# Second biases of a dense feed-forward: one f32 product of 9 rows, or one bf16 product of 96 rows with nine pairs of parts

## The chip, the cores and the metric

The kernel runs on one core of one Trainium2 chip. The metric is the device time of one execution in microseconds (us), as the median of several runs. The core has five engines that work side by side and meet at semaphores: TensorE (PE; its weight loads are listed apart as PEld), VectorE (DVE), ScalarE (ACT), GpSimd (POOL) and SyncE (SP, which here issues the transfers).

## The reference

The whole reference is a chain of six residual steps on x of 8 x 512 x 256 in f32: an expert feed-forward, an attention, the expert feed-forward again, then a dense feed-forward, a second attention, and the dense feed-forward again. The change lies in the dense feed-forward alone, which is run twice with the same weights (E = 8 experts, H = 128, D = 256, K = 2):

```python
scores = jax.nn.sigmoid(x @ gate_W) * route_scale
topk_scores, topk_idx = jax.lax.top_k(scores, K)
topk_w = topk_scores / topk_scores.sum(-1, keepdims=True)
gate_full = jnp.einsum('bsk,bske->bse', topk_w, jax.nn.one_hot(topk_idx, E))
h = jax.nn.gelu(jnp.einsum('bsd,edh->bseh', x, W1) + b1, approximate=False)
y = jnp.einsum('bseh,ehd->bsed', h, W2) + b2
expert_out = jnp.einsum('bse,bsed->bsd', gate_full, y)
shared = jax.nn.gelu(x @ Ws1 + bs1, approximate=False) @ Ws2 + bs2
return expert_out + shared
```

It is called as `x = x + 0.5 * ffn(layernorm(x))`. Every expert is computed for every token and weighted by its gate, which is zero for six of the eight. What matters here is the term of the second biases: for each token, the sum over experts of gate times `b2`, and the shared expert's `bs2`.

## The kernel before, in words

The residual x stays in on-chip memory (`core.x`) throughout. The kernel is a row of phases, one for each step of the reference, each a block with an instruction list for each engine; a barrier of all engines stands between two phases. The dense feed-forward is `ffn1_phase`, the fourth and the last phase. Phase A below is its first run, phase B the second.

A phase takes the 8 batches of 512 tokens in turn. The loop runs over pairs of batches, with two buffers (k = 0, 1) for what is kept per batch. The shared expert counts as a ninth (NE = 9), and `RUN` puts it first. In the loop TensorE does this for each n from 0 to 8:

- `up`: two f32 products of 128 x 512 for the next expert (L299), on which ScalarE applies gelu (L360);
- `down`: four f32 products of 128 x 256 for expert n (L311), one for each tile of 128 tokens, into two halves of the buffers `y_ps`. There are four such buffers, so TensorE can be two experts ahead of VectorE; `y_free` says which are free;
- between them: at n = 2 `turn_gates`, four transposes of the batch's gates (L289); at n = 4 and 5 the transposes of the next batch's normalised x (L164); at n = 6 the next batch's gate logits (L281).

After n = 8 come the `biases` (L324): for each tile of tokens one product of the turned gates (9 rows) with `b2_sb` (9 rows: b2, and bs2 with the gate 0.5), and then the first `up` of the next batch.

VectorE adds each y, times its gate, to x: `add(n)` (L428 for four tiles, L422 for the shared expert and the biases, two halves each). Behind `add(0)` it takes the statistics of the next batch, behind `add(2)` it copies the turned gates out of the accumulator (L411) and normalises the next batch (L149, L152), behind `add(4)` and `add(5)` it copies its transposes (L176), behind `add(7)` it computes its gates (L384 to L406). `add(8)` and `add(9)`, the biases, close the batch. Instructions of an engine run in the order of its list.

Ahead of the loop SP issues all loads of weights (L246 to L258), VectorE normalises batch 0 and computes its gates, `gates(0, 0)`, and TensorE makes the transposes, the first `up` and the logits of batch 0, then waits for the loads and enters the loop. Also in the last batch of a phase the work for the next batch is done, on spare tiles, and nothing of it is used.

Of the kernel before, what the change touches and what calls it, by code (L numbers as in the profile page):

```python
# [185 lines left out]
def ffn1_phase(core, name, gate_w, w1, b1, w2, b2, ws1, bs1, ws2, bs2, route_scale, out_dram=None):  # L186

    nc = core.nc  # L190
# [4 lines left out]
    YB = 4  # L195
    ctx = ExitStack()
    with ctx:
# [8 lines left out]
        b2_sb = sb("b2", [NE, D])  # L206
# [11 lines left out]
        gate_t = [sb(f"gate_t{k}", [NE, S]) for k in range(2)]  # L218
# [11 lines left out]
        const_ready = sem("const_ready")  # L230
        logits_ready = sem("logits_ready")
        sig_ready = sem("sig_ready")
        gate_ready = sem("gate_ready")
# [11 lines left out]
        def _(sp):  # L245
# [11 lines left out]
            sp.dma_start(b2_sb[0:E, :], b2).then_inc(down_loaded, 16)  # L257
            sp.dma_start(b2_sb[E:NE, :], bs2.rearrange("(o d) -> o d", o=1)).then_inc(down_loaded, 16)  # L258
# [6 lines left out]
        @block.gpsimd  # L265
        def _(pool):
            nc.gpsimd.iota(iota_e[:, :, :], pattern=[[0, TPB], [1, E]], base=0, channel_multiplier=0,
                           allow_small_or_imprecise_dtypes=True)
            for k in range(2):
                last = nc.gpsimd.memset(gate[k][:, :, E:NE], 0.5)  # L270
            last.then_inc(const_ready, 1)

        @block.tensor
        def _(pe):
# [11 lines left out]
            def turn_gates(i, k):  # L286
                pe.wait_ge(gate_ready, i + 1)
                for j in range(TPB):
                    last = nc.tensor.transpose(gate_ps[0:NE, j * P:(j + 1) * P], gate[k][:, j, :],  # L289
                                               core.ident[:, :])  # L290
                last.then_inc(gate_t_ready, 1)
# [25 lines left out]
            def biases(i, k):  # L317
                pe.wait_ge(gate_t_copied, i + 1)
                for half in range(2):
                    m = 2 * NE + half  # L320
                    pe.wait_ge(y_free, i * UNITS + m + 1)
                    for j in range(2):
                        t = 2 * half + j
                        last = nc.tensor.matmul(y_ps[m % YB][:, j, :], gate_t[k][:, t * P:(t + 1) * P],  # L324
                                                b2_sb[:, :], start=True, stop=True)
                    last.then_inc(y_ready, 1)
# [7 lines left out]
            pe.wait_ge(down_loaded, 64)  # L334
            with pe.Fori(0, B // 2) as pair:
                for k in range(2):
                    i = pair * 2 + k
                    for n in range(NE):
                        if n + 1 < NE:
                            up(i, k, n + 1)  # L340
                        down(i, k, n)
                        if n == 2:
                            turn_gates(i, k)
                        if n in (4, 5):
                            norm.pe_transpose(i + 1, chunks=(n - 4,))
                        if n == 6:
                            logits(i + 1, 1 - k)
                    biases(i, k)
                    up(i + 1, 1 - k, 0)
# [30 lines left out]
        def _(dve):  # L380
            def gates(i, k):
# [20 lines left out]
                for r in range(2):  # L402
# [4 lines left out]
                                        ALU.add).then_inc(gate_ready, 1)  # L407

            def copy_gates(i, k):
                dve.wait_ge(gate_t_ready, i + 1)  # L410
                nc.vector.tensor_copy(gate_t[k][:, :], gate_ps[0:NE, :]).then_inc(gate_t_copied, 1)  # L411
# [29 lines left out]
            gates(0, 0)  # L441
            for i in range(1, B):
                core.wait_x(dve, i)
            with dve.Fori(0, B // 2) as pair:
                for k in range(2):
                    i = pair * 2 + k
                    for n in range(NE + 1):
                        add(i, k, n)
                        if n == 0:
                            norm.dve_stats(i + 1)  # L450
                        if n == 2:
                            copy_gates(i, k)
                            norm.dve_normalise(i + 1)
                        if n in (4, 5):
# [2220 lines left out]
```

## Time and profile before

| | |
|---|---|
| median of 3 runs | 3226.8 us (3223.7 to 3229.19) |
| profiled execution, its own time | 3219.98 us |
| its span, first to last instruction | 3218.2 us |
| mean granted TensorE clock | 0.947 of full |
| busy share of the span: PE, PEld | 90%, 64% |
| busy share: DVE, ACT, POOL | 51%, 47%, 42% |
| start of phase A, of phase B (first load issued) | 2018.22 us, 2904.87 us |

A busy share is an average over six phases with different limits; the place of the change is the last phase and the fourth. Times in the rows below are microseconds from the span's start, unless marked as ns. An f32 product stands in the trace as two records on PE.

### The profile page before, as it was taken

To read this page: it belongs to the slowest core of one execution; us is meant where nothing else is said; L and a number is where in the kernel's file an instruction comes from. 1 tells how busy PE (TensorE), PEld (TensorE's weight loads), DVE (VectorE), ACT (ScalarE), POOL (GpSimd) and SP (SyncE) were. 2 spreads that over 40 slices of the span, in tenths; PEclk is the share of its full clock that TensorE was granted. 3 is DMA by queue.
4 is the path that set the end of the run, shared out by engine and by line. 5 is a ranking of instruction groups with operands and counts; after the bars stand their busy time and mean duration, and the time that the engine had idled before them with its cause. 6 is when DMAs were issued, how large, how long until landed. Compare 5 with 4: busy or idle time off the path is not lost. (4 is left out here: it accounts for less than half of the span.)

```text
span 3218.2 us, 53908 instructions
## 1 busy us (share of the span) xinstructions
PE 2896.9 (90%) x19497; PEld 2067.5 (64%) x19497; DVE 1649.1 (51%) x4513; ACT 1527.6 (47%) x2577; POOL 1346.6 (42%) x1333
## 2 busy tenths in 40 slices
PE   5899999768999999568999999899969999998999
PEld 4799999733444443247999998566635666655666
DVE  4411111168888888455111111566676666665666
ACT  1133333249988888410333332233347777772332
POOL 3444444359989888335344443000043344320000
PEclk9899999989999999757999999899989999998999
DMA  7199999713544444641899997200052233301000
GB/s 278 40 302 317 321 316 319 239 30 20 61 60 60 59 59 60 94 168 53 262 319 321 322 313 236 82 0 0 8 142 72 70 88 95 95 2 37 13 13 20
DMA packets 354987, 431.81 MB, mean 134 GB/s; under 512 B 84528, under 2 KB 312771, under 8 KB 350659
## 3 DMA queue, kind: packets, MB, share of 16 engines
q1 hardware_dynamic: 330178, 395.16, 44.2%
q0 software_dynamic: 24576, 33.57, 4.8%
q8 instruction: 144, 2.36, 0.3%
q14 instruction: 89, 0.72, 0.1%
HBM read 355.80 MB, written 72.88 MB: 133 GB/s over the span
## 5 line engine op out<-in xcount | busy, mean ns | idle before, releaser
L1674 ACT ACTIVATE f_h_t<-f_h_ps,f_b_t 128x128 f32<-128x128 f32 x1024 | 320.4, 364 | 617.1 <-PE f_h_ps L1633 617.1
L2041 POOL TENSOR_TENSOR a_dmg_buf<-a_c 128x2048 f32<-128x2048 f32 x128 | 520.1, 4096 | 65.6 <-PE a_dmg_ps L2088 43.9
L1633 PEld LDWEIGHTS f_h_ps<-f_rows_t,f_w 128*128 128x128 f32 x4096 | 481.5, 193 | 9.9 <-issue 3.5
L1633 PE MATMUL f_h_ps<-f_rows_t,f_w 128*128 128x128 f32 x4096 | 482.6, 276 | 2.3 <-DVE f_rows_t L1686 1.2
L1644 PE MATMUL f_y_ps<-f_w,f_h_t 128*128 128x256 f32 x2048 | 462.9, 379 | 0.0
L1593 POOL DMA_INDIRECT acc_rows<-f_y,f_give x128 | 205.0, 1602 | 509.1 <-DMA acc_rows<-f_y,f_give 372.1
L1644 PEld LDWEIGHTS f_y_ps<-f_w,f_h_t 128*128 128x128 f32 x2048 | 379.3, 190 | 46.4
L2373 DVE SCALAR_TENSOR_TENSOR a_bond_buf<-a_a,a_small_rep,a_q_ps 128x512 f32<-128x512 f32 x512 | 346.9, 741 | 36.8 <-PE a_bond_ps L2088 35.1
L428 DVE SCALAR_TENSOR_TENSOR x_resid<-f_y_ps,f_gate,x_resid 128x256 f32 x512 | 218.7, 479 | 162.5 <-PE f_y_ps L311 156.9
L885 ACT ACTIVATE a_prob<-a_prob,a_neg_top 128x384 f32<-128x384 f32 (+3 forms) x512 | 276.5, 570 | 47.3 <-POOL a_neg_top L702 46.9
L299 PE MATMUL f_h_ps<-f_xn_t,f_w 128*128 128x512 f32 x584 | 282.5, 611 | 3.3 <-DVE f_xn_t L176 1.8
L998 DVE CUSTOM_DVE_ANT_0 a_prob<-a_s_ps,a_factor 128x384 f32<-128x384 f32 (+3 forms) x512 | 234.4, 486 | 86.5 <-PE a_s_ps L779 84.5
L360 ACT ACTIVATE f_h_t<-f_h_ps,f_b 128x512 f32<-128x512 f32 x146 | 100.3, 687 | 368.6 <-PE f_h_ps L299 368.3
L311 PEld LDWEIGHTS f_y_ps<-f_w,f_h_t 128*128 128x128 f32 x1152 | 219.6, 191 | 86.2 <-issue 55.1
L311 PE MATMUL f_y_ps<-f_w,f_h_t 128*128 128x256 f32 x1152 | 270.5, 380 | 0.1
L1686 DVE COPY f_rows_t<-f_t_ps 128x256 f32<-128x256 f32 x128 | 54.4, 425 | 408.4 <-PE f_t_ps L1621 408.4
L2309 ACT ACTIVATE a_dmg_buf<-a_dmg_buf,a_small_rep 128x2048 f32<-128x2048 f32 x128 | 255.2, 1994 | 4.9 <-POOL a_dmg_buf L2041 4.8
L2304 ACT ACTIVATE a_bond_buf<-a_bond_buf,a_bond_act_b 128x2048 f32<-128x2048 f32 x128 | 255.5, 1996 | 2.0 <-DVE a_bond_buf L2373 1.8
L1693 DVE TENSOR_TENSOR f_y_biased<-f_y_ps,f_b 128x256 f32<-128x256 f32 x128 | 54.4, 425 | 393.4 <-PE f_y_ps L1644 381.3
L790 PE MATMUL a_t_ps<-ident,a_prob 128*128 128x128 f32 x1280 | 231.1, 280 | 17.6 <-ACT a_prob_t L896 13.5
L896 ACT COPY a_prob_t<-a_t_ps 128x512 f32<-128x512 f32 (+1 forms) x352 | 192.8, 548 | 100.7 <-PE a_t_ps L790 99.5
L702 POOL TENSOR_SCALAR a_neg_top<-a_top 128x1 f32<-128x1 f32 x512 | 105.1, 209 | 323.5 <-DVE a_top L998 298.5
(333 smaller groups left out, 4274.5 us busy)
## 6 DMA issues: line engine op xcount, KB each, us to landing
f_w<-in_L_ffn_w_dram SPq DMA_DIRECT2D x256, 1024.0 KB
a_skewed<-skew SPq DMA_DIRECT2D x8, 2048.0 KB, 8.4
a_k_s<-parts SPq DMA_DIRECT2D x16, 768.0 KB, 7.8
acc_rows<-x_resid SPq DMA_DIRECT2D x17, 512.0 KB, 4.5
xn_rows<-f_xn SPq DMA_DIRECT2D x16, 512.0 KB, 3.0
x_resid<-acc_rows SPq DMA_DIRECT2D x16, 512.0 KB, 7.5
a_vals<-val_rows SPq DMA_DIRECT2D x64, 128.0 KB, 5.3
skew<-a_bond SPq DMA_DIRECT2D x32, 256.0 KB
```

Source lines behind the costliest of these rows:

```text
L299: last = nc.tensor.matmul(h_ps[(k * NE + n) % 2][:, :], w1_sb[:, RUN[n], c, :], norm.xn_t[k][:, c, :], start=c == 0, stop=c == DC - 1)
L311: last = nc.tensor.matmul(y_ps[m % YB][:, j, :], h[:, t * P:(t + 1) * P], w2_sb[:, RUN[n], :], start=True, stop=True)
L790: last = nc.tensor.transpose(t_ps[pack % TB][:, col + kb * P:col + (kb + 1) * P], prob[:, u % PR, kb * P:(kb + 1) * P], core.ident[:, :])
L885: nc.scalar.activation(prob[:, u % PR, 0:width], prob[:, u % PR, 0:width], ACT.Exp, bias=neg_top[:, u % PR:u % PR + 1]).then_inc(exp_ready, 1)
L998: nc.vector.tensor_tensor_reduce(out=prob[:, u % PR, 0:width], in0=s_ps[use % SB][:, 0:width], in1=factor[:, S - width:S], scale=1.0, scal ...
L1633: last = nc.tensor.matmul(h_ps[n // HB][:, (n % HB) * P:(n % HB + 1) * P], w1_sb[s][:, c, n * P:(n + 1) * P], rows_t[e % 2][:, c, :], star ...
L1644: last = nc.tensor.matmul(y_ps[k][:, 0:D], h_t[k][:, n, :], w2_sb[e % R][:, n, :], start=n == 0, stop=n == HC - 1)
L1674: nc.scalar.activation(h_t[k][:, n, :], h_ps[n // HB][:, (n % HB) * P:(n % HB + 1) * P], ACT.Gelu, bias=b1_t[:, n, e:e + 1]).then_inc(gelu ...
L2041: nc.gpsimd.tensor_tensor(dmg_buf[n % RING][:, :, :], places(c_sb[h], first_place(dg)), c_sb[h][:, PAD:].unsqueeze(1).broadcast_to([P, DG, ...
L2304: nc.scalar.activation(buf[:, :, :], buf[:, :, :], ACT.Gelu, bias=bond_act_b[:, h:h + 1]).then_inc(bond_act, 1)
L2309: nc.scalar.activation(buf[:, :, :], buf[:, :, :], ACT.Gelu, bias=small_rep[:, B_DAMAGE:B_DAMAGE + 1]).then_inc(dmg_act, 1)
L2373: last = nc.vector.scalar_tensor_tensor(out=bond_buf[n % RING][:, dd, :], in0=a_sb[h][:, d + 1:d + 1 + S], scalar=small_rep[:, POS + d:POS ...
```

## The change

The bias product is made in bf16. An f32 number is the sum of three bf16 parts (the rounded number, the rounded rest, the rest of that), and the product of a gate and a bias is the sum of nine products of parts. These nine pairs are laid out as rows of one product: group m of 32 rows holds part m of the biases, three times over (27 rows, 5 of zeros), and in `gate_parts` each group has the three parts of the gates. So the product has 96 rows in the place of 9. What this asks for:

- SP: b2 and bs2 are loaded nine times each, 18 loads in the place of 2, behind a wait for GpSimd, which first sets `b2_sb` to zero (and `gate_parts`).
- VectorE, once per phase, behind `gates(0, 0)`: `split_biases`, which waits for the 18 loads and makes `b2_rows` in seven operations. TensorE waits for it ahead of the loop.
- VectorE, per batch: `split_first` behind the statistics at n = 0 and `split_second` at n = 1, seven operations on 36 or 108 columns.
- TensorE: `turn_gates` transposes 96 columns in the place of 9, at n = 3 in the place of n = 2; the copy L411 moves to n = 3 with it and writes bf16.

```diff
-        b2_sb = sb("b2", [NE, D])
+        b2_sb = sb("b2", [PROWS, D])
+        b2_rest = sb("b2_rest", [PROWS, D])
+        b2_part = sb("b2_part", [PROWS, D], BF16)
+        b2_rows = sb("b2_rows", [PROWS, D], BF16)
...
-            sp.dma_start(b2_sb[0:E, :], b2).then_inc(down_loaded, 16)
-            sp.dma_start(b2_sb[E:NE, :], bs2.rearrange("(o d) -> o d", o=1)).then_inc(down_loaded, 16)
+            sp.wait_ge(b2_cleared, 1)
+            for m in range(PARTS):
+                for l in range(PARTS):
+                    row = 32 * m + NE * l
+                    sp.dma_start(b2_sb[row:row + E, :], b2).then_inc(b2_loaded, 16)
+                    sp.dma_start(b2_sb[row + E:row + NE, :], bs2.rearrange("(o d) -> o d", o=1)).then_inc(b2_loaded, 16)
...
+            nc.gpsimd.memset(b2_sb[:, :], 0.0).then_inc(b2_cleared, 1)
+            nc.gpsimd.memset(gate_parts[:, :, :], 0.0)
...
-            def turn_gates(i, k):
-                pe.wait_ge(gate_ready, i + 1)
+            def turn_gates(i):
+                pe.wait_ge(parts_ready, i + 1)
                 for j in range(TPB):
-                    last = nc.tensor.transpose(gate_ps[0:NE, j * P:(j + 1) * P], gate[k][:, j, :],
+                    last = nc.tensor.transpose(gate_ps[0:PROWS, j * P:(j + 1) * P], gate_parts[:, j, :],
                                                core.ident[:, :])
...
-                        last = nc.tensor.matmul(y_ps[m % YB][:, j, :], gate_t[k][:, t * P:(t + 1) * P],
-                                                b2_sb[:, :], start=True, stop=True)
+                        last = nc.tensor.matmul(y_ps[m % YB][:, j, :], gate_t[:, t * P:(t + 1) * P],
+                                                b2_rows[:, :], start=True, stop=True)
...
-            pe.wait_ge(down_loaded, 64)
+            pe.wait_ge(down_loaded, 32)
+            pe.wait_ge(b2_split, 1)
...
-                        if n == 2:
-                            turn_gates(i, k)
+                        if n == 3:
+                            turn_gates(i)
...
-            def copy_gates(i, k):
+            def copy_gates(i):
                 dve.wait_ge(gate_t_ready, i + 1)
-                nc.vector.tensor_copy(gate_t[k][:, :], gate_ps[0:NE, :]).then_inc(gate_t_copied, 1)
+                nc.vector.tensor_copy(gate_t[:, :], gate_ps[0:PROWS, :]).then_inc(gate_t_copied, 1)
+
+            def split_biases():
+                dve.wait_ge(b2_loaded, 32 * PARTS * PARTS)
+                nc.vector.tensor_copy(b2_part[:, :], b2_sb[:, :])
+                nc.vector.drain()
+                nc.vector.tensor_copy(b2_rows[0:32, :], b2_part[0:32, :])
+                nc.vector.tensor_tensor(b2_rest[:, :], b2_sb[:, :], b2_part[:, :], ALU.subtract)
+                nc.vector.drain()
+                nc.vector.tensor_copy(b2_part[:, :], b2_rest[:, :])
+                nc.vector.drain()
+                nc.vector.tensor_copy(b2_rows[32:64, :], b2_part[32:64, :])
+                nc.vector.tensor_tensor(b2_rest[:, :], b2_rest[:, :], b2_part[:, :], ALU.subtract)
+                nc.vector.drain()
+                nc.vector.tensor_copy(b2_rows[64:PROWS, :], b2_rest[64:PROWS, :]).then_inc(b2_split, 1)
+
+            def split_first(k):
+                nc.vector.tensor_copy(gate_part[0][:, :, :], gate[k][:, :, :])
+                nc.vector.drain()
+                nc.vector.tensor_tensor(gate_rest[:, :, :], gate[k][:, :, :], gate_part[0][:, :, :], ALU.subtract)
+                nc.vector.tensor_copy(place_part(0), across(gate_part[0][:, :, :]))
+                nc.vector.drain()
+                nc.vector.tensor_copy(gate_part[1][:, :, :], gate_rest[:, :, :])
+
+            def split_second():
+                nc.vector.drain()
+                nc.vector.tensor_tensor(place_part(2), across(gate_rest[:, :, :]), across(gate_part[1][:, :, :]), ALU.subtract)
+                nc.vector.tensor_copy(place_part(1), across(gate_part[1][:, :, :])).then_inc(parts_ready, 1)
...
             gates(0, 0)
+            split_biases()
...
                         if n == 0:
                             norm.dve_stats(i + 1)
+                        if n == 0:
+                            split_first(k)
+                        if n == 1:
+                            split_second()
                         if n == 2:
-                            copy_gates(i, k)
                             norm.dve_normalise(i + 1)
+                        if n == 3:
+                            copy_gates(i)
```

`place_part(l)` is the place of part l in all three groups of `gate_parts`, `across` repeats a part over the groups; PARTS = 3 and PROWS = 96.

## Rows read from the trace of the kernel before

**Rows 1.** The page: granted TensorE clock in 40 equal slices, in tenths

```profile
PEclk9899999989999999757999999899989999998999
```

**Rows 2.** The page: the chain that ended last, shares of the span by line

```profile
PE f_h_ps L299 4%; PE f_y_ps L311 4%; PE f_gate_ps L281 1%; PE f_y_ps L324 0%; PE f_tp L164 0%; PE f_gate_ps L289 0%; DVE x_resid L428 0%; DVE f_xn_t L176 0%; DVE f_xn L152 0%; DVEq L458 0%; DVE f_stats L134 0%; DVEq L415 0%; DVE f_top_i L390 0%; DVEq L385 0%; DVEq L135 0%
```

**Rows 3.** Windows: length, busy by engine (instructions), granted clock, DMA share, GB/s

```profile
2920.00:2926.00 6.00, 5.91 (x11) 2.92 (x11) 2.46 (x23) 4.14 (x5) 0.00 (x0) 0.53 0.00 0
2119.80:2156.00 36.20, 36.20 (x146) 24.68 (x145) 23.76 (x76) 11.72 (x15) 0.00 (x0) 1.00 0.00 0
```

**Rows 4.** Timeline, turn of a batch: start, duration, engine, line, shapes, count, idle before

```profile
2069.10 1.99 PE L324 MATMUL f_y_ps<-f_b,f_gate_t 9*128 9x256 f32 x8
...
2071.02 3.70 PE L299 MATMUL f_h_ps<-f_xn_t,f_w 128*128 128x512 f32 x8
...
2073.14 1.29 DVE L422 SCALAR_TENSOR_TENSOR x_resid<-f_y_ps,x_resid 128x512 f32 x2 [0.17 <-issue]
...
2074.56 1.89 PE L311 MATMUL f_y_ps<-f_w,f_h_t 128*128 128x256 f32 x8
```

**Rows 5.** Timeline, the last batch of phase B

```profile
3213.01 1.29 DVE L422 SCALAR_TENSOR_TENSOR x_resid<-f_y_ps,x_resid 128x512 f32 x2 [0.17 <-issue]
```

**Rows 6.** Timeline, the start of phase A (SPq: SP issues a transfer)

```profile
2027.10 2.11 SPq L257 DMA_DIRECT2D f_b<-in_L_ffn_b_dram  x1
2027.36 0.17 POOL L267 IOTA f_iota_e<- 128x32 f32 x1 [19.20 <-issue]
...
2029.25 0.25 SPq L258 DMA_DIRECT2D f_b<-in_L_ffn_bs_dram  x1
...
2034.97 3.54 PE L299 MATMUL f_h_ps<-f_xn_t,f_w 128*128 128x512 f32 x4 [1.58 <-DMA f_b<-in_L_ffn_bs_dram]
...
2037.78 0.19 DVE L406 TENSOR_TENSOR f_gate<-f_part 128x32 f32<-128x32 f32 x1
```

**Rows 7.** Timeline, the start of phase B

```profile
2911.47 0.25 SPq L258 DMA_DIRECT2D f_b<-in_L_ffn_bs_dram  x1
...
2919.88 3.76 PE L299 MATMUL f_h_ps<-f_xn_t,f_w 128*128 128x512 f32 x4
...
2924.41 0.19 DVE L406 TENSOR_TENSOR f_gate<-f_part 128x32 f32<-128x32 f32 x1
```

**Rows 8.** Timeline, bf16 products and a bf16 weight load of other phases

```profile
1510.79 0.49 PE L1329 MATMUL f_pos_ps<-f_pick,f_before 128*128 128x256 bf16 x3
...
1511.11 0.67 PE L1333 MATMUL f_pos_ps<-f_pick,f_ones 128*128 128x192 bf16 x9
...
2600.84 0.10 PEld L777 LDWEIGHTS a_s_ps<-a_k_s,a_q_s 96*128 96x128 bf16 x1
```

**Rows 9.** Timeline, VectorE: first and last of seven splitting operations; four of L152

```profile
24.87 0.18 DVE L1431 CAST f_gate_b_part<-f_gate_b 3x64 bf16<-3x64 f32 x1 [5.41 <-DMA f_gate_b<-in_L_ffn_gate_b_dram]
...
26.32 0.27 DVE L1442 SCALAR_TENSOR_TENSOR f_gate_b_rows<-f_gate_b_rest,ident,f_gate_b_sum 3x64 bf16<-3x64 f32 x1
...
2084.99 1.38 DVE L152 TENSOR_SCALAR f_xn<-x_resid,f_mean_var,f_rstd 128x256 f32 x4
```

**Rows 10.** Timeline, VectorE at n = 2 of the second batch

```profile
2082.51 1.74 DVE L428 SCALAR_TENSOR_TENSOR x_resid<-f_y_ps,f_gate,x_resid 128x256 f32 x4 [1.48 <-PE f_y_ps L311]
```

**Rows 11.** One of ten small loads in a row; landing times of L246; the DMA list

```profile
644.93 0.42 SPq L1931 DMA_DIRECT2D a_small<-in_L_attn_w_damage_dram  x1
```

```profile
DMA to landing us min/median/max: 2.1/4.7/7.3
```

```profile
f_b<-in_L_ffn_bs_dram SPq DMA_DIRECT2D x2, 0.5 KB, 4.1
```

**Rows 12.** Timeline, four transposes with 9 and with 128 columns of weights

```profile
2046.96 0.60 PE L289 MATMUL f_gate_ps<-ident,f_gate 128*9 128x128 f32 x4
...
2054.29 0.60 PE L164 MATMUL f_tp<-ident,f_xn 128*128 128x128 f32 x4
```

**Rows 13.** Timeline, the start of the first expert's products

```profile
148.42 6.46 PE L1633 MATMUL f_h_ps<-f_rows_t,f_w 128*128 128x128 f32 x32 [0.61 <-DVE f_rows_t L1686]
```

More of the change, by code:

```diff
@@ L195, in ffn1_phase @@
     YB = 4
+    PARTS = 3
+    PROWS = 32 * PARTS
     ctx = ExitStack()
@@ L217, in ffn1_phase @@
         gate = [sb(f"gate{k}", [P, TPB, NE]) for k in range(2)]
-        gate_t = [sb(f"gate_t{k}", [NE, S]) for k in range(2)]
+        gate_part = [sb(f"gate_part{l}", [P, TPB, NE], BF16) for l in range(2)]
+        gate_rest = sb("gate_rest", [P, TPB, NE])
+        gate_parts = sb("gate_parts", [P, TPB, PROWS])
+        gate_t = sb("gate_t", [PROWS, S], BF16)
         h_t = [sb(f"h_t{k}", [P, S]) for k in range(2)]
@@ L230, in ffn1_phase @@
         const_ready = sem("const_ready")
+        b2_cleared = sem("b2_cleared")
+        b2_loaded = sem("b2_loaded")
+        b2_split = sem("b2_split")
+        parts_ready = sem("parts_ready")
         logits_ready = sem("logits_ready")
         sig_ready = sem("sig_ready")
-        gate_ready = sem("gate_ready")
         gate_t_ready = sem("gate_t_ready")
@@ L406, in gates @@
                 nc.vector.tensor_tensor(gate[k][:, :, 0:E], part[0][:, :, :], part[1][:, :, :],
-                                        ALU.add).then_inc(gate_ready, 1)
-            def copy_gates(i, k):
+                                        ALU.add)
+            def copy_gates(i):
                 dve.wait_ge(gate_t_ready, i + 1)
-                nc.vector.tensor_copy(gate_t[k][:, :], gate_ps[0:NE, :]).then_inc(gate_t_copied, 1)
+                nc.vector.tensor_copy(gate_t[:, :], gate_ps[0:PROWS, :]).then_inc(gate_t_copied, 1)
@@ new lines, in place_part, with across @@
+            def place_part(l):
+                return gate_parts[:, :, :].rearrange("p j (m r) -> p j m r", m=PARTS)[:, :, :, l * NE:(l + 1) * NE]
+            def across(part):
+                return part.unsqueeze(2).broadcast_to([P, TPB, PARTS, NE])
+            def split_first(k):
[5 more added lines that the diff above has]
+                nc.vector.tensor_copy(gate_part[1][:, :, :], gate_rest[:, :, :])
```

## The prediction

> **What bounds the kernel now.** I read the page first. The granted clock of TensorE is at nine or ten tenths in almost all slices [rows 1], and the chain that ended last is made of TensorE lines: L299 and L311 with 4% each, L281 with 1%, and L324, the bias product, below that [rows 2]. This chain is the last phase only. A barrier stands ahead of each phase, so a feed-forward phase counts in full, and there are two dense ones: phase A from 2018 us and phase B from 2905 us.
>
> Then the windows: over one batch of 36.2 us TensorE is busy for all 36.20 us at full clock, VectorE for 23.76 us and ScalarE for 11.72 us [rows 3]. Inside the loop the path is TensorE's own work, and the others have slack. Outside it are two places that the averages hide: the start of each phase, where the loop waits for loads or runs straight on, and the end, where VectorE finishes. So the timeline is needed for three stretches: the turn from one batch to the next [rows 4], the last additions [rows 5] and the two starts [rows 6, 7].
>
> **1. The bias products themselves (a gain).** L324 starts at 2069.10 and the next products (L299) at 2071.02, so the block takes 1.92 us: eight records, since an f32 product is two [rows 4]. In bf16 with 96 rows it is four. The bf16 product nearest to it in the trace has 256 columns as well: three of L1329 start at 1510.79 and the next line at 1511.11, 0.11 us each [rows 8]. The two waits in the block leave about 0.2 us (1.92 less 8 x 0.215, the pace of L311, 1.73 us for eight starts in the same rows). So 4 x 0.11 + 0.2 = 0.64 us, and the gain is 1.28 us. Bounds: if each weight load of 0.10 us [rows 8] stood ahead of its product, 1.04 us, a gain of 0.88; if the waits vanish too, 0.44 us, a gain of 1.48. The shortest reading is no surer than the longest, so I take the middle.
>
> How often does it count? In all batches but the last of each phase. There VectorE closes: its chain add(7), gates, add(8), add(9) doesn't start from the bias product but from add(7), and add(9) begins at 3213.01 right behind add(8), with 0.17 us of issue and no wait for TensorE [rows 5]. Biases that are ready 1.3 us sooner end nothing sooner. So 14 batches, not 16: 14 x 1.28 = **17.9 us gained** (12.3 to 20.7).
>
> At the turn the pipeline must also follow. VectorE ends add(9) at 2074.43 and now gets its next product from L311, which starts at 2074.56 [rows 4]; 1.28 us sooner it has the first half ready at about 2074.2, so VectorE starts some 0.3 us behind its data. TensorE doesn't wait for that, because it may run two experts ahead (four y_ps buffers, two per expert): over 4 us of lead.
>
> **2. Turning the gates.** Four transposes with 96 columns of weights in the place of 9. Four transposes with 128 take 0.60 us, as do the four with 9 [rows 12]: nothing. Moving them from n = 2 to n = 3 moves the same work to the same engine: nothing, as long as the split is done by then. The copy at L411 has the same 512 columns, and goes behind add(3) with them.
>
> **3. VectorE's splitting in the loop.** Seven small operations and three more waits for the pipeline to drain. The trace has their like: the three parts of the expert gate's bias, seven operations on 64 columns, take from 24.87 to 26.59, 1.7 us [rows 9], so some 1.5 us per batch: about 0.9 behind the statistics at n = 0 and 0.6 at n = 1. VectorE has 12 us idle per batch [rows 3], but at n = 0 and 1 it is already late. It waits again at n = 2, for 1.48 us [rows 10], so a lag of 1.5 us is used up there, and n = 2 has lost its gate copy. The cover is the lead of over 4 us; I put the cost at **0** (0 to 1). Were the cover gone, each further us per batch would cost 14.
>
> **4. The start of each phase (a loss).** The loop now waits on TensorE for b2_split: 18 loads in SP's queue instead of 2, then a split that stands in VectorE's queue behind gates(0, 0). Nothing overlaps it, since TensorE's queue has only the loop behind the wait. SP waits for a memset on GpSimd ahead of the loads. If that is as late as GpSimd's first instruction in A is now, 2027.36, it costs 0.6 us against 2027.10, when SP comes to the loads [rows 6]; if it runs at the phase's start, nothing, which I take.
>
> - *Loads.* In A the first pair is issued at 2027.10 (2.11 us, behind the large weights) and 2029.25 [rows 6]. Small loads in a row take 0.42 us each [rows 11] and 0.04 between two, as behind the first pair, 0.46 us, so the last begins at 2029.25 + 16 x 0.46 = 2036.6. Landing: between 2.1 us, the least of L246, and 4.1 us, the median of the small f_b load [rows 11]; I take 3.0, hence 2039.6. In B: 2911.47 + 7.4 + 3.0 = 2921.8 [rows 7].
> - *A page beside it.* The Trainium skill ("DMA: Bandwidth & Descriptors", the section on the anatomy of one DMA) gives a fixed cost of about 2.0 us per transfer. By it A's last load lands at 2038.6, and the whole change would come out 1 us better, as an estimate; the 4.1 us of the row speaks for more.
> - *Gates.* They end at 2037.97 in A [rows 6] and 2924.60 in B [rows 7]. So A waits for the loads, B for VectorE.
> - *Split.* Seven operations on 256 columns with four drains. The 1.7 us above is for 64 columns; a 256-column operation takes 0.345 us (L152, 1.38 for four [rows 9]) and would make 7 x 0.345 + 0.3 = 2.7 us; casts and copies may be cheaper. I take 2.6 (1.8 to 3.0), with 0.2 us of semaphores in all.
> - *Sum.* A: 2039.6 + 2.8 = 2042.4, where the loop starts at 2034.97 today [rows 6]: 7.4 us lost. With loads at 0.29 us each the gates end last: 2037.97 + 0.2 + 1.8, 5.0 us lost; with 4.1 us of landing and 3.0 of split 8.9. B: 2924.6 + 2.8 = 2927.4, where it starts at 2919.88 without a wait: 7.5 us lost (6.7 to 8.0). **14.9 us lost** (11.7 to 16.9).
>
> **5. The clock at the start.** The granted clock is 0.53 in B from 2920 to 2926 [rows 3], mostly the lower level of 1.2 GHz, and the four L299 records at the start take 3.54 us in A [rows 6] and 3.76 in B [rows 7] against half that in the loop. TensorE runs below its level for some 3 us in A and 6 us in B before it rises, so today this costs about 1.5 + 3 = 4.5 us. It will stand idle longer, and start again at the lower level: the idle stretch takes nothing more, but the rise may come sooner or later. Another dense start has 32 records of 128 columns in 6.46 us [rows 13], 0.20 us each, where 256 columns take 0.215 in the loop: 6.5 us at the lower level, a cost of 3.2. Twice 1.5 to twice 3.2 against 4.5: **0** taken, -1.5 to +1.9.
>
> **Sum.** -17.9 + 14.9 + 0 + 0 = -3.0 us. On the profiled execution, 3219.98 us (span 3218.2), this gives 3217.0. The median of the runs is 6.8 us above that execution, so I add the difference to the median: 3226.8 - 3.0 = **3223.8 us**. All ends on one side: -20.7 + 11.7 - 1.5 = -10.5, 3216.3; on the other -12.3 + 16.9 + 1.9 + 1 = +7.5, 3234.3. A measurement of this kernel can tell about 0.2%, 6.5 us, from no change.
>
> **Rivals.**
> - *Faster: the loads and the split are short, and the products retire without breaks.* 14 x 1.48 = 20.7 gained, 5.0 + 6.7 lost: -9.0, 3217.8 us. For it: the last load of a row is issued in 0.25 us, and casts may be quick. Against it: the b2 loads sit in a row of loads, where 0.46 us is the rule. Chance 0.17.
> - *Slower: SP's issue of b2.* L257 takes 2.11 us in A [rows 6]. I read it as a queue still full of weights. If it is its own cost, and only 1.4 of it stays, eight further pairs take 1.4 + 0.3 each: the last is issued at 2029.25 + 13.6 = 2042.9 in A and at 2925.1 in B, and with the same 3.0 and 2.8 us behind it the loop starts at 2048.7 and 2930.9: 13.7 and 11.0 us lost. 24.7 - 17.9 = +6.8, 3233.6 us. It decides from about 1.4 us for each b2 load. Against it: small loads of many rows in rows 11 take 0.42. Chance 0.09.
> - *VectorE becomes the bound at n = 1 to 3.* Needs a lag over 4 us, three times what I find; at half a us per batch over that, +7 on my sum: 3231. Chance 0.03.
> - *The bf16 products cost what the f32 ones do.* Then only the loss is left: 3241.7. Rows 8 speak against it. Chance 0.02.
>
> **How the numbers follow.** My forecast holds 0.69. It spreads from 3218 to 3231 by itself, with some of that below the bound for faster and little above the one for slower. Faster: 0.17 and 0.03 of mine, 0.20. Slower: 0.09 + 0.02 + 0.01, 0.12. Same: 0.68. Range: from the faster rival to the SP rival, 3217 to 3233.5.
>
> **What the profile after would show.** L324 with 64 records in all, bf16, 96 rows, and 0.6 to 0.7 us from it to the next L299; a batch of 34.9 us; 16 more SP issues at about 0.46 us; the loop's first L299 at 24 us after A's first issue (2018.2) where it is 16.8 now, and 22.5 after B's (2904.9) where it is 15.0; add(0) right behind add(9); no wait of TensorE for x_resid at n = 2 or 3. I am wrong if the batch is not near 34.9 us, if a start costs more than 10 us, or if TensorE waits for parts_ready.

## The result and the profile after

| | median | lowest to highest | runs |
|---|---|---|---|
| before | 3223.22 us | 3213.24 to 3231.72 | 20 |
| changed | 3211.81 us | 3200.91 to 3223.45 | 20 |

The ratio is 0.9965 with a 95% interval of 0.9953 to 0.9976. By the ratio that is 11.3 us less (7.7 to 15.2), more than the 0.2% that can be told from no change. The forecast was 3223.8 us, from 3217.0 to 3233.5, with 0.68 on no change. Of the 12.0 us between forecast and result, 3.6 come from the base, since 20 runs put the kernel before at 3223.2 and not at 3226.8. The other 8.4 are the change itself: the medians differ by 11.4 where 3.0 was said. The profiled execution took 3202.66 us, with a span of 3200.9.

The page of the changed kernel, part 4, answers to [rows 2]: the chain is still TensorE's, and the bias product (L344) has sunk within it from fourth to sixth place.

```profile
PE f_h_ps L319 4%; PE f_y_ps L331 4%; PE f_gate_ps L301 0%; PE f_tp L164 0%; PE f_gate_ps L309 0%; PE f_y_ps L344 0%; DVE x_resid L483 0%; DVE f_xn_t L176 0%; DVE f_xn L152 0%; DVE f_top_i L411 0%; DVEq L519 0%; DVE f_stats L134 0%; DVEq L470 0%; DVE f_top_v L408 0%; DVEq L445 0%
```

**The turn of a batch.** The timeline of TensorE over the same turn as [rows 4], then its weight loads.

```profile
2065.55 3.62 PE L331 MATMUL f_y_ps<-f_w,f_h_t 128*128 128x256 f32 x16
2069.00 0.60 PE L344 MATMUL f_y_ps<-f_b_rows,f_gate_t 96*128 96x256 bf16 x4
2069.44 3.60 PE L319 MATMUL f_h_ps<-f_xn_t,f_w 128*128 128x512 f32 x8
2072.88 1.89 PE L331 MATMUL f_y_ps<-f_w,f_h_t 128*128 128x256 f32 x8
```

```profile
2065.55 3.21 PEld L331 LDWEIGHTS f_y_ps<-f_w,f_h_t 128*128 128x128 f32 x15 [0.24 <-issue]
2068.79 0.53 PEld L344 LDWEIGHTS f_y_ps<-f_b_rows,f_gate_t 96*128 96x128 bf16 x4
2069.33 0.30 PEld L319 LDWEIGHTS f_h_ps<-f_xn_t,f_w 128*128 128x128 f32 x2
```

The same stretch of the kernel before, in rows that the first part did not show: the last products ahead of the biases, and the weight loads around them.

```profile
2065.56 3.62 PE L311 MATMUL f_y_ps<-f_w,f_h_t 128*128 128x256 f32 x16
```

```profile
2069.10 1.59 PEld L324 LDWEIGHTS f_y_ps<-f_b,f_gate_t 9*128 9x128 f32 x8 [0.33 <-issue]
2071.02 0.30 PEld L299 LDWEIGHTS f_h_ps<-f_xn_t,f_w 128*128 128x128 f32 x2 [0.33 <-issue]
```

Compare starts, not durations. Before, the steps from the last L311 block to the biases, to L299 and to the next L311 are 3.54, 1.92 and 3.54 us. After, they are 3.45, 0.44 and 3.44. The block itself fell by 1.48 us, and each neighbour is 0.1 us shorter as well, which together makes 1.67. The weight loads show the border. The first bias load used to begin with its own product at 2069.10 after 0.33 us of idle, and now begins 0.21 us ahead of it, with no idle. The next line's load used to have another 0.33 us ahead of it, and that is gone as well. The other seven loads of the old block had none: over all 128 loads of L324 the trace of the kernel before counts 16 such idles, 5.3 us, one for each of the 16 blocks. So the cost stands where the number of rows changes, from 128 to 9 and back, and not at each load of 9 rows.

The period confirms it. Here is the timeline of the next two bias blocks, and the window over one batch (length, busy by engine, granted clock, as in [rows 3]):

```profile
2103.54 0.60 PE L344 MATMUL f_y_ps<-f_b_rows,f_gate_t 96*128 96x256 bf16 x4
2138.07 0.60 PE L344 MATMUL f_y_ps<-f_b_rows,f_gate_t 96*128 96x256 bf16 x4
```

```profile
2133.50:2168.04 34.54, 34.54 (x141) 23.78 (x141) 24.61 (x81) 11.72 (x16) 0.00 (x0) 1.00 0.00 0
```

The bias blocks follow each other at 34.53 and 34.54 us throughout both phases, where they followed at 36.21 before. TensorE is busy for the whole of a batch, so nothing in it waits for VectorE, though VectorE has 0.85 us more work (24.61 against 23.76).

VectorE at the same turn and at n = 0 to 2: the additions follow one another, the splitting lies between them, and the third addition no longer waits 1.48 us for TensorE as in [rows 10].

```profile
2073.11 1.29 DVE L477 SCALAR_TENSOR_TENSOR x_resid<-f_y_ps,x_resid 128x512 f32 x2 [0.17 <-issue]
2074.67 1.29 DVE L477 SCALAR_TENSOR_TENSOR x_resid<-f_y_ps,x_resid 128x512 f32 x2 [0.28 <-issue]
...
2077.89 0.17 DVE L456 CAST f_gate_part<-f_gate 128x36 bf16<-128x36 f32 x1
...
2078.53 0.18 DVE L461 CAST f_gate_part<-f_gate_rest 128x36 bf16<-128x36 f32 x1
...
2080.63 0.27 DVE L465 TENSOR_TENSOR f_gate_parts<-f_gate_rest,f_gate_part 128x108 f32<-128x108 f32 x1
2080.81 0.21 DVE L466 CAST f_gate_parts<-f_gate_part 128x108 f32<-128x108 bf16 x1
2081.19 1.66 DVE L483 SCALAR_TENSOR_TENSOR x_resid<-f_y_ps,f_gate,x_resid 128x256 f32 x4 [0.16 <-issue]
```

**The start of phase A** (first issue at 2013.54), to be held against [rows 6]: the first two and the last of the eighteen loads, the logits block, the end of gates(0, 0), the first and the last of the seven splitting operations, and the loop's first products.

```profile
2013.54 0.37 SPq L259 DMA_DIRECT2D f_w<-in_L_ffn_Ws_dram  x1
2013.55 0.31 POOL L285 MEMSET f_b<- 96x256 f32 x1 [10.69 <-POOLq L51]
...
2021.90 1.40 SPq L274 DMA_DIRECT2D f_b<-in_L_ffn_b_dram  x1
...
2023.64 0.27 SPq L274 DMA_DIRECT2D f_b<-in_L_ffn_b_dram  x1
...
2025.24 1.85 PE L301 MATMUL f_gate_ps<-f_gate_w,f_xn_t 128*128 128x8 f32 x16
...
2028.21 0.25 SPq L275 DMA_DIRECT2D f_b<-in_L_ffn_bs_dram  x1
...
2031.48 0.19 DVE L427 TENSOR_TENSOR f_gate<-f_part 128x32 f32<-128x32 f32 x1
2031.59 0.28 DVE L436 CAST f_b_part<-f_b 96x256 bf16<-96x256 f32 x1
...
2033.65 0.28 DVE L446 CAST f_b_rows<-f_b_rest 32x256 bf16<-32x256 f32 x1
2034.29 3.77 PE L319 MATMUL f_h_ps<-f_xn_t,f_w 128*128 128x512 f32 x4 [7.19 <-DVE f_b_rows L446]
```

The load rows show that the loads are not what the loop waits for. From the second pair on they take 0.27 and 0.25 us, the last is issued at 2028.21, and the split begins at 2031.59, right behind the gates. TensorE's wait of 7.19 us is released by the last splitting operation. The loop starts 20.75 us after the phase's first issue here and 16.8 us after it before. Phase B does the same, as its timeline shows beside [rows 7]:

```profile
2894.55 0.39 SPq L259 DMA_DIRECT2D f_w<-in_L_ffn_Ws_dram  x1
...
2912.47 0.19 DVE L427 TENSOR_TENSOR f_gate<-f_part 128x32 f32<-128x32 f32 x1
...
2915.28 3.78 PE L319 MATMUL f_h_ps<-f_xn_t,f_w 128*128 128x512 f32 x4 [7.36 <-DVE f_b_rows L446]
```

**The balance.** From the first issue of phase A to that of the phase behind it is 310.8 us before and 303.7 after. From the first issue of phase B to the end of the span it is 313.3 and 306.3. So the two phases gave 14.1 us in this profile. The terms are 14 x 1.67 = 23.4 gained, 4.0 and 5.7 lost at the starts, and 0.3 gained between the loop's start and its steady pace. The span fell by 17.3. The other 3.2 us lie in code that the change doesn't touch, and are scatter of the profiled executions.

### The profile page after: what moved, and what is told of

It is laid out like the page before. It is cut to its first block and busy times, and to the rows that moved or that the text cites. A ratio compares the mean times of both kernels' runs of the same rounds, so it can differ in the third digit from the quotient of the medians.

```text
span 3200.9 us, 53982 instructions
## 1 busy us (share of the span) xinstructions
PE 2868.0 (90%) x19433; PEld 2047.2 (64%) x19433; DVE 1667.3 (52%) x4623; ACT 1526.7 (48%) x2577; POOL 1348.1 (42%) x1337
## 5 line engine op out<-in xcount | busy, mean ns | idle before, releaser
L319 PE MATMUL f_h_ps<-f_xn_t,f_w 128*128 128x512 f32 x584 | 280.8, 608 | 16.3 <-DVE f_b_rows L446 14.6
L851 PE MATMUL a_t_ps<-ident,a_prob 128*128 128x128 f32 x1280 | 232.4, 281 | 17.3 <-ACT a_prob_t L957 13.3
```

Source lines behind the costliest of these rows:

```text
L319: last = nc.tensor.matmul(h_ps[(k * NE + n) % 2][:, :], w1_sb[:, RUN[n], c, :], norm.xn_t[k][:, c, :], start=c == 0, stop=c == DC - 1)
L851: last = nc.tensor.transpose(t_ps[pack % TB][:, col + kb * P:col + (kb + 1) * P], prob[:, u % PR, kb * P:(kb + 1) * P], core.ident[:, :])
```

## The experiments

Ahead of each result stands what was expected of it. The first four ran on one chip, where one run of the kernel before took 3232.81 us.

**after_again.** The changed kernel once more, with no edit, to see how far two of its executions differ.

> The changed kernel once more, for what varies by itself. Inside a phase the batch should be 34.54 us again and the loop should start 20.7 us after the phase's first issue. Theory 1: the logits ahead of the loop ran at full clock by the luck of when the clock rose (block of 16 records 1.85 us where it was 3.42 before): then the block may take either length here, and the loop's start lies between 20.7 and 22.4. Theory 2: it belongs to the change: 1.85 again in both phases.

It took 3214.08 us. The period is 34.53 to 34.54 us again, so the gain in the loop is the same. The starts are not: the loop begins 22.4 us after A's first issue (at 2023.70) and 22.5 after B's (at 2903.94), 1.6 and 1.8 us later than in the first profile. Its timeline at B's start:

```profile
2915.68 3.42 PE L301 MATMUL f_gate_ps<-f_gate_w,f_xn_t 128*128 128x8 f32 x16
...
2923.65 0.19 DVE L427 TENSOR_TENSOR f_gate<-f_part 128x32 f32<-128x32 f32 x1
...
2926.45 3.78 PE L319 MATMUL f_h_ps<-f_xn_t,f_w 128*128 128x512 f32 x4 [7.35 <-DVE f_b_rows L446]
```

The windows over the logits block of phase B, in the first profile of the changed kernel and then in this one, give the reason in the column behind the five engines, the granted clock (0.92 in the first, 0.50 in the second):

```profile
2906.40:2909.80 3.40, 1.52 (x14) 1.42 (x13) 0.17 (x1) 1.77 (x3) 0.00 (x0) 0.92 0.00 1
```

```profile
2915.70:2919.10 3.40, 3.40 (x17) 3.31 (x15) 0.00 (x0) 0.00 (x0) 0.00 (x0) 0.50 0.02 3
```

The block takes 1.85 us when the clock has reached its upper level (2.4 GHz) before it, and 3.42 us at the lower one (1.2 GHz). In the 14 profiles of this study, with two phase starts each, the block took at most 2.3 us in 13 of the 28. It came out both ways for the same code, as the first theory had it: this kernel had it short twice and long twice. Since the split now stands behind the gates, and the gates behind the logits, those 1.6 us move the loop's start. At the lower clock the starts lose 5.6 us in A and 7.5 in B (22.4 - 16.8 and 22.5 - 15.0), which is like against like, since the kernel before had 3.42 in both phases. The value for A is less sure than the one for B. In the six profiles here of kernels with two bias loads and no split (the kernel before and those with 32 to 128 rows in f32), the loop begins 15.3 to 17.8 us after A's first issue, because TensorE waits there for loads, and they land at different times. The two phases together gave 10.4 us in this profile.

**rows96_f32.** The kernel before with the biases and the turned gates widened to 96 rows, 87 of them zero, still in f32 and with two loads. GpSimd sets the tiles to zero at the phase's start, and the two loads wait for that.

```diff
-        b2_sb = sb("b2", [NE, D])
+        b2_sb = sb("b2", [96, D])
-        gate = [sb(f"gate{k}", [P, TPB, NE]) for k in range(2)]
-        gate_t = [sb(f"gate_t{k}", [NE, S]) for k in range(2)]
+        gate = [sb(f"gate{k}", [P, TPB, 96]) for k in range(2)]
+        gate_t = [sb(f"gate_t{k}", [96, S]) for k in range(2)]
...
-                    last = nc.tensor.transpose(gate_ps[0:NE, j * P:(j + 1) * P], gate[k][:, j, :],
+                    last = nc.tensor.transpose(gate_ps[0:96, j * P:(j + 1) * P], gate[k][:, j, :],
```

> The kernel before, in f32, with gates and biases padded by zeros from 9 rows to 96. Theory rows: the 9-row product was slow at its borders, some 0.1 us ahead of it and 0.1 behind it and again behind the first load of the next product; with 96 rows this goes and the batch falls from 36.21 to 35.9 us. Theory type: the rest of the gain (1.67 per batch where 1.28 was forecast) comes from four bf16 records in the place of eight: the batch stays 36.21 us.

It took 3227.81 us, with a period of 35.82 to 35.83: 0.39 us less per batch for rows of zeros alone. The theory of the rows holds, at 35.82 us where it said 35.9. Its turn, products and weight loads:

```profile
2079.42 3.62 PE L318 MATMUL f_y_ps<-f_w,f_h_t 128*128 128x256 f32 x16
2082.87 1.89 PE L331 MATMUL f_y_ps<-f_b,f_gate_t 96*128 96x256 f32 x8
2084.60 1.88 PE L306 MATMUL f_h_ps<-f_xn_t,f_w 128*128 128x512 f32 x4
```

```profile
2082.66 1.70 PEld L331 LDWEIGHTS f_y_ps<-f_b,f_gate_t 96*128 96x128 f32 x8
2084.38 0.41 PEld L306 LDWEIGHTS f_h_ps<-f_xn_t,f_w 128*128 128x128 f32 x2
```

The eight records now take 1.73 us from start to start and not 1.92, the block begins 3.45 us behind the last L318 block and not 3.54, and both idle 0.33 us ahead of the loads are gone. Here the part of the gain that the rows make is alone.

**rows9_bf16.** The kernel before with the two operands of the bias product in bf16, nine rows. It leaves out the second and third parts of both, so its biases are rounded to bf16.

```diff
-        gate_t = [sb(f"gate_t{k}", [NE, S]) for k in range(2)]
+        gate_t = [sb(f"gate_t{k}", [NE, S], BF16) for k in range(2)]
+        b2_rows = sb("b2_rows", [NE, D], BF16)
...
+            pe.wait_ge(b2_split, 1)
...
+            dve.wait_ge(down_loaded, 64)
+            nc.vector.tensor_copy(b2_rows[:, :], b2_sb[:, :]).then_inc(b2_split, 1)
```

> The kernel before with the 9-row product in bf16, on the first part of gates and biases alone: the second and third parts are left out. Two loads, one cast of the biases. Theory rows: the borders stay slow, so a batch of 34.85 us. Theory type: 34.54 us, as with 96 rows. The loop should start less than 1 us later than before, against the first issue of the phase.

It took 3217.94 us, with a period of 34.83. Its turn:

```profile
2078.99 3.62 PE L313 MATMUL f_y_ps<-f_w,f_h_t 128*128 128x256 f32 x16
2082.53 0.60 PE L326 MATMUL f_y_ps<-f_b_rows,f_gate_t 9*128 9x256 bf16 x4
2083.07 3.70 PE L301 MATMUL f_h_ps<-f_xn_t,f_w 128*128 128x512 f32 x8
```

```profile
2082.53 0.33 PEld L326 LDWEIGHTS f_y_ps<-f_b_rows,f_gate_t 9*128 9x128 bf16 x4 [0.33 <-issue]
2083.07 0.30 PEld L301 LDWEIGHTS f_h_ps<-f_xn_t,f_w 128*128 128x128 f32 x2 [0.21 <-issue]
```

So the type alone gives 36.21 - 34.83 = 1.38 us, and at nine rows the 0.33 us ahead of the first load is back. From here to the changed kernel's 34.54, the 96 rows give 0.29. The start was expected less than 1 us later than before, and that was wrong: in B, with the logits block at 3.42 us as before, this kernel's loop begins 20.3 us after the first issue and not 15.0. It has two loads, and one cast of 0.27 us behind the gates instead of a split. So 5.3 of B's 7.5 us are lost by standing behind the gates at all, and only 2.2 by the split.

**loads18.** The kernel before with the eighteen loads, and TensorE's wait for all of them, and nothing else of the change. `b2_sb` is 96 rows high to hold them, and the product reads its first nine.

```diff
-            sp.dma_start(b2_sb[0:E, :], b2).then_inc(down_loaded, 16)
-            sp.dma_start(b2_sb[E:NE, :], bs2.rearrange("(o d) -> o d", o=1)).then_inc(down_loaded, 16)
+            for m in range(3):
+                for l in range(3):
+                    row = 32 * m + NE * l
+                    sp.dma_start(b2_sb[row:row + E, :], b2).then_inc(down_loaded, 16)
+                    sp.dma_start(b2_sb[row + E:row + NE, :], bs2.rearrange("(o d) -> o d", o=1)).then_inc(down_loaded, 16)
...
-            pe.wait_ge(down_loaded, 64)
+            pe.wait_ge(down_loaded, 32 + 32 * 9)
```

> The kernel before with the 18 loads of the changed one and its 9-row f32 product: the loads alone, no split; TensorE waits for all 18 ahead of the loop. If a b2 load is issued in 0.27 us as in the changed kernel, the last is issued at about 10.3 to 15 us after the phase's first issue and lands some 2.5 us on: the loop starts at 15.0 in B as before and at 16.8 to 17.8 in A. With my forecast's 0.46 us each it would start at 21.4 in A and 17.0 in B. Batch 36.21 us in either case.

It took 3236.72 us; the period is 36.21. The loop begins 17.9 us after A's first issue and 14.8 after B's, and in both phases TensorE waits for the last load, 2.69 us in A and 1.14 in B:

```profile
2937.98 3.34 PE L302 MATMUL f_h_ps<-f_xn_t,f_w 128*128 128x512 f32 x4 [1.14 <-DMA f_b<-in_L_ffn_bs_dram]
```

The 14.8 us in B cannot be set against the 15.0 of before, since the logits block took 1.89 us here and 3.42 there. The kernels with two loads and a short block in B begin the loop at 13.4 or 13.5 us (rows32_f32, rows64_of96 and rows96_f32_timed, below). So the loads cost some 1.3 us in B where the clock has risen, and nothing where it has not, as an estimate, since the last one has landed at 14.8. In A, 17.9 us lies at the upper edge of the 15.3 to 17.8 of the kernels with two loads: a cost of up to 2.6 us, which one profile can't narrow. Behind the gates, where the changed kernel waits, none of this shows.

**late_wait.** The changed kernel with TensorE's wait for the split moved from ahead of the loop into the bias step.

```diff
             def biases(i, k):
+                pe.wait_ge(b2_split, 1)
                 pe.wait_ge(gate_t_copied, i + 1)
...
-            pe.wait_ge(b2_split, 1)
             with pe.Fori(0, B // 2) as pair:
```

> The changed kernel with one wait moved: TensorE waits for b2_split ahead of the bias product of each batch and not ahead of the loop. Theory: what the start lost (5.6 us in A and 7.5 in B where the logits ran at the low level) was TensorE idle behind gates and split, and VectorE being late there is covered by the two experts of lead: the loop starts at about 15 to 16.5 us in both phases, the batch stays 34.54, and the time falls by some 12 us against the changed kernel, to about 0.993 of the kernel before. Rival: VectorE, late by the 2.3 us of the split, stops TensorE at the third expert, and half or more of the gain goes.

The median of six runs, beside 16 of the kernel before on the same chip (median 3232.97 us), is 3205.48: a ratio of 0.9928, from 0.9902 to 0.9954. Its timeline at B's start, with products and VectorE together:

```profile
2914.86 3.42 PE L301 MATMUL f_gate_ps<-f_gate_w,f_xn_t 128*128 128x8 f32 x16
2918.14 3.76 PE L319 MATMUL f_h_ps<-f_xn_t,f_w 128*128 128x512 f32 x4
...
2925.01 0.28 DVE L446 CAST f_b_rows<-f_b_rest 32x256 bf16<-32x256 f32 x1
...
2925.80 1.29 DVE L477 SCALAR_TENSOR_TENSOR x_resid<-f_y_ps,x_resid 128x512 f32 x2 [0.51 <-issue]
```

TensorE goes from the logits straight into the loop, 15.0 us after the first issue as before the change, while VectorE is still at gates and split. In A it begins after 15.5 us, and what it waits for there is a load of weights. The two phases last 299.2 and 301.7 us, 23.3 less than the 310.8 and 313.3 of before, and that is 14 x 1.67. The whole loss at the start is gone, and VectorE's delay of 2.3 us ahead of its first addition costs nothing.

**pool_split.** late_wait, with the seven splitting operations on GpSimd, each waiting for the one before, and not on VectorE.

```diff
+            pool.wait_ge(b2_loaded, 32 * PARTS * PARTS)
...
+            done(nc.gpsimd.tensor_copy(b2_part[:, :], b2_sb[:, :]))
+            done(nc.gpsimd.tensor_copy(b2_rows[0:32, :], b2_part[0:32, :]))
...
-            split_biases()
```

> As late_wait, and the seven splitting operations stand on GpSimd, each behind the last. Theory: VectorE's lateness in the first batch cost nothing, so the time is that of late_wait within 1 us. Rival: VectorE's 2.3 us at the start are felt by TensorE, and this is 2 to 4 us faster than late_wait.

The median of six runs is 3209.70 us, a ratio of 0.9935, from 0.9914 to 0.9956. Its phases last 298.9 and 301.7 us, as those of late_wait do within 0.3 us. It cannot be told from late_wait: once TensorE doesn't wait for the split, it doesn't matter which engine makes it.

**rows96_f32_timed.** The kernel of rows96_f32 again, in twelve runs on the same chip as those two.

> The f32 kernel with gates and biases padded to 96 rows of which 87 are zeros, timed. 14 times 0.39 us is 5.5 us less per kernel, no loss at the start: about 0.998 of the kernel before. If only the profile were faster: 1.000.

3225.13 us, a ratio of 0.9977, from 0.9962 to 0.9991. The lower end is 12.3 us and the upper 2.9, and 14 x 0.39 = 5.5 lies between. The padding with zeros makes this kernel faster, by its times as well as by its period.

**rows32_f32 and rows128_f32.** rows96_f32 with 32 and with 128 in the place of 96, to find where the border vanishes.

> The f32 kernel padded to 32 rows. Where does the slow border end? If it is a matter of a weight load that fills no whole quarter of the array's rows, 32 rows are enough and the batch is 35.82 us as with 96. If it is a matter of how many quarters the load has against its neighbours of 128, it is as slow as with 9 rows, 36.21 us.

> The f32 kernel padded to 128 rows. If 96 rows have left nothing of the border, 35.82 us per batch again; if each quarter of rows counts, some 0.1 us less.

They took 3244.99 and 3231.41 us, beside 3239.43 for one run of the kernel before. Single runs differ by more than the 5.5 us in question, so the period decides. With 32 rows the period is 36.21 and nothing is gained; with 128 it is 35.82, as with 96. The weight loads of the kernel with 32 rows have both idle 0.33 us, as with nine:

```profile
2092.23 1.59 PEld L331 LDWEIGHTS f_y_ps<-f_b,f_gate_t 32*128 32x128 f32 x8 [0.33 <-issue]
2094.15 0.30 PEld L306 LDWEIGHTS f_h_ps<-f_xn_t,f_w 128*128 128x128 f32 x2 [0.33 <-issue]
```

**rows64_of96.** rows96_f32 with its memory and its transposes at 96, and the product over the first 64 rows alone. Transposes of 64 columns were not measured.

```diff
-                        last = nc.tensor.matmul(y_ps[m % YB][:, j, :], gate_t[k][:, t * P:(t + 1) * P],
-                                                b2_sb[:, :], start=True, stop=True)
+                        last = nc.tensor.matmul(y_ps[m % YB][:, j, :], gate_t[k][0:64, t * P:(t + 1) * P],
+                                                b2_sb[0:64, :], start=True, stop=True)
```

> The f32 kernel with gates turned at 96 columns and the bias product on the first 64 of the 96 rows. 32 rows gave 36.21 us (slow), 96 gave 35.82. If the slow border belongs to loads of a single quarter of the array's rows, 35.82; if to loads of no more than half, 36.21; a value between would say that it shrinks by quarters.

3230.49 us, with a period of 36.21 and the idle in its old place:

```profile
2077.77 1.59 PEld L331 LDWEIGHTS f_y_ps<-f_b,f_gate_t 64*128 64x128 f32 x8 [0.33 <-issue]
2079.69 0.30 PEld L306 LDWEIGHTS f_h_ps<-f_xn_t,f_w 128*128 128x128 f32 x2 [0.33 <-issue]
```

So it is the rows of the product itself, not the width of the transposes, and the step lies between 64 and 96 rows.

**split_twice.** The changed kernel with the first splitting of the gates done twice in each batch, four operations and three drains more on VectorE.

```diff
                             split_first(k)
+                            nc.vector.drain()
+                            split_first(k)
```

> The changed kernel with split_first done twice in each batch, some 1.0 us more on VectorE at n = 0. Theory: the splitting in the loop lies under TensorE's lead and costs nothing, so the batch stays 34.54 us. Rival: VectorE is at the edge (it no longer waits at n = 2) and a batch grows by up to 1.0 us.

It took 3220.28 us beside 3239.43. The period is 34.53 to 34.54 as without it, though VectorE is busy for 25.29 us of a batch and not for 24.61. VectorE's splitting in the loop costs nothing, and 0.7 us more of it still costs nothing.

**late_wait_f32_96.** In spite of its name this is late_wait unchanged, in four runs on another chip.

> The kernel of late_wait again, timed against the kernel before on another chip: 0.993 of it, in 0.990 to 0.996, and a batch of 34.54 us.

The median is 3204.16 us against 3232.16, a ratio of 0.9922, from 0.9903 to 0.9941. The period is 34.53 to 34.54 us, and the phases last 299.6 and 301.4. The version with the later wait beats the kernel before on both chips, and this interval lies wholly below that of the change as it was made.

## Why the prediction was wrong

The sum had the right terms and the right signs, and two of them had the wrong size. Both errors made the forecast too slow.

**Step 1, the bias products: the step that failed.** The gain of 1.28 us per batch was mis-sized, and so was its upper bound of 1.48; it measured 1.67, and the batch fell to 34.54 us where 34.9 was said. The term took the 0.2 us by which the old block exceeded the pace of L311 as the cost of its semaphore waits, and kept it. But rows96_f32 has the same waits and eight records in 1.73 us, so the waits cost nothing. The 0.2 us belong to the two changes in the number of rows, at the block's start and at its end, and 96 rows remove them. Another 0.2 lay outside the block, in the 3.54 us on each side of it, where the time from L324 to L299 alone does not show it. Fourteen times 0.39 is 5.5 us, the whole miss of this term (23.4 against 17.9). Of the 0.39 that were missed per batch, 0.29 are the rows (34.83 to 34.54), which the forecast put at nothing. The other 0.10 is the type: 1.38 measured at nine rows against 8 x 0.215 - 4 x 0.11 = 1.28, since half of the block's 0.2 goes with the type already (1.92 to 0.54 us in rows9_bf16).

**How often it counts: right.** Fourteen, not sixteen. after_again ties it: 310.8 - 7 x 1.67 + 5.6 = 304.7 us for phase A, and 305.3 were measured; eight would give 303.0. The 0.6 us between lie at the start: TensorE took 5.7 us from the loop's start to its second block of L319 there, and 5.1 to that of L299 before. late_wait's 23.3 us are 14.0 times 1.67. VectorE still closes, with an addition of its own right behind another, as in [rows 5]:

```profile
3195.68 1.29 DVE L477 SCALAR_TENSOR_TENSOR x_resid<-f_y_ps,x_resid 128x512 f32 x2 [0.17 <-issue]
```

**Steps 2 and 3, transposes and splitting at no cost: right.** rows64_of96 has the wide transposes and the old period; split_twice leaves 34.54 us. The lag that was foreseen is there (the second addition comes right behind the first), and the 1.48 us of idle at n = 2 absorbed it.

**Step 4, the start: right in B, mis-sized in A.** 7.5 us in B was measured as 7.5 at the same clock; 7.4 in A as 5.6, against one profile of a start that varies by itself. In A the loads were to end last, at 0.46 us each. They took 0.27 and 0.25, with 0.04 between, so they landed before the gates were done and both phases waited for gates and split: 2.62 us from the end of the gates to the loop, where 2.8 was said. The landing time never came to decide. In loads18, where it does, the loop begins 2.7 us (A) and 3.4 us (B) after the issue of the last load, near the 3.0 that was taken. The 2.0 us that the prediction sets beside it stand in the Trainium skill ("DMA: Bandwidth & Descriptors", the section on the anatomy of one DMA) for transfers that GpSimd issues. These are SP's, and both measured times are longer. The forecast's lower bound for A, 5.0, had this case in it. What it did not see is how the loss divides: 5.3 of B's 7.5 us are the place of the wait, behind the gates, and the rest is the split. Moving one line takes both away.

**Step 5, the clock at the start: right on average.** From the loop's start to its second block of L319 or L299 products took 5.78 us in A and 5.61 in B after, and 5.11 and 6.59 before: -0.3 us in all. But the clock has a second effect that the step missed. It sets the logits block, 1.85 or 3.42 us, and the changed kernel's loop waits for what comes behind it. The first profile had both short and so lost 4.0 and 5.7, the second both long.

**The sum again.** -23.4 + 5.6 + 7.5 = -10.3 us at the lower clock, beside a measured -11.3 (-15.2 to -7.7), and -14.1 and -10.4 for the two phases together in the two profiles. The gain term accounts for 5.5 of the 8.4 us of error, the start for 1.8 (14.9 against 13.1); the remaining 1.1 is within the interval. Of the rivals the faster one came nearest. Its mechanisms were both right (short loads, products that retire without breaks). Its gain of 20.7 us lacked only the part outside the block, and its loss of 11.7 was 1.4 us short of the 13.1 at the lower clock. It had 0.17, because the 0.46 us between loads was taken as the rule. The SP rival needed 1.4 us for each b2 load, and only the first took that; VectorE never became the bound, and the bf16 products did not cost what the f32 ones do.

## What to carry to other kernels

When a block of small products is replaced, measure from the start of the block ahead to the start of the second block behind it, and read the weight loads of both kernels too: a cost at the border belongs to neither line. A wait that guards something used 35 us later belongs where it is used; ahead of the loop it put TensorE behind another engine's whole chain for 4.0 to 7.5 us a phase, and a line moved gave it back. And where the surplus of a block is put down to waits, ask what else could make it before keeping it in the sum.

## What the runs showed of the hardware

**The first weight load behind a change to few rows, or back, is not taken ahead.** Behind products with 128 rows, the first load with 9, 32 or 64 rows began only with its own product, with 0.33 us of idle ahead of it, and the next load with 128 rows stood behind an idle too (0.33 us in f32, 0.21 where the block is bf16). With 96 and 128 rows it began 0.21 us ahead. Inside the block the further loads of 9 rows had no idle (16 idles for the 128 loads of L324). Each block with its two changes cost 0.39 us in f32 (36.21 against 35.82) and 0.29 in bf16 (34.83 against 34.54). The Trainium skill ("TensorE: Matmul & The Clock Gate", the mechanism in the part on packing small matmuls) says that a load is pulled ahead of running products when its row groups don't conflict with theirs or it goes to the background weight buffer. By that condition alone, loads with 9 and with 96 rows, both among rows that the running products use, would behave alike. The traces differ from that here (0.33 us of idle against none). Why the step lies between 64 and 96 rows stays open, and no size between them was tried.

**Small loads differ in their issue.** Eight rows of b2 (8 KB) took 0.27 us of SP and one row 0.25, where the small loads of [rows 11] take 0.42; the first of them behind the large weights took 1.40 us in A and 0.98 in B in the changed kernel, 2.11 in A before, and 0.55 in B in loads18.
